# Order of the drain work on four engines of a two-layer transformer kernel, and weight columns that are loaded into another buffer

## What is computed

```
x = x + _L0_attn_ref(_layernorm(x), q_kernel, kv_kernel, out_kernel, q_norm_scale, k_norm_scale)
x = x + _L0_ffn_ref(_layernorm(x), w_gate, w_up, w_down)
x = x + _L1_attn_ref(_layernorm(x), W_K, W_Q, W_V, W_O)
x = x + _L1_ffn_ref(_layernorm(x), W1, W2, W3)
```

## Time and profile before

| | |
|---|---|
| median of 3 runs | 732.27 us (732.14 to 892.83) |
| profiled execution, time | 732.23 us |
| profiled execution, span from first to last instruction | 730.4 us |
| PE busy | 704.2 us, 96% of the span |
| DVE busy | 496.1 us, 68% |
| ACT busy | 403.7 us, 55% |
| POOL busy | 359.0 us, 49% |
| granted TensorE clock | 1.00 |
| DMA | 34 GB/s mean |

### The profile page before, as it was taken

The page is one execution under the profiler, slowest core; times in us unless marked ns, Lnnn a source line. Parts: engine busy times, 40 slices in busy tenths (PEclk is TensorE's granted clock), DMA queues, the critical chain, the costliest instruction groups (busy, mean ns, idle before and its releaser), DMA issues.

```text
span 730.4 us, 14854 instructions
## 1 busy us (share of the span) xinstructions
PE 704.2 (96%) x4296; PEld 628.6 (86%) x4296; DVE 496.1 (68%) x1698; ACT 403.7 (55%) x1205; POOL 359.0 (49%) x508
## 2 busy tenths in 40 slices
PE   4799999999999998999999999999999999999998
PEld 3589999999999987888879999999999999878887
DVE  6998888888888898768757454444445444567443
ACT  4576666666676663523246555555555555554221
POOL 3898888888887884002179342323232325317000
PEclk9999999999999999999999999999999999999999
DMA  6010110101020021100011010101101100000000
GB/s 230 1 44 2 44 45 1 43 0 43 0 101 29 0 87 73 44 1 1 15 59 59 1 59 3 57 14 45 33 25 51 49 0 14 0 15 1 1 30 29
DMA packets 9002, 24.64 MB, mean 34 GB/s; under 512 B 896, under 2 KB 3072, under 8 KB 8832
## 3 DMA queue, kind: packets, MB, share of 16 engines
q1 hardware_dynamic: 8240, 22.55, 8.9%
q10 hardware_dynamic: 720, 1.57, 0.6%
HBM read 23.07 MB, written 1.05 MB: 33 GB/s over the span
## 4 chain that ended last, share of the span: by engine, by line
PE 90%; DVE 6%; issue 1%; POOL 1%; DMA 1%; ACT 1%; DVEq 0%; POOLq 0%; ACTq 0%
PE bank L620 12%; PE bank L309 12%; PE bank L328 11%; PE bank L303 11%; PE bank L360 8%; PE bank L281 7%; PE bank L340 6%; PE bank L349 5%; PE bank L362 4%; PE bank L280 4%; PE bank L371 3%; PE bank L663 2%; PE bank L659 2%; PE bank L687 1%; DVE probs L445 1%
## 5 line engine op out<-in xcount | busy, mean ns | idle before, releaser
L433 ACT ACTIVATE probs<-scores,negmax 128x128 f32<-128x128 f32 (+1 forms) x256 | 115.6, 452 | 43.1 <-DVE negmax L481 42.4
L462 DVE TENSOR_TENSOR enc_lo<-bank,enc_hi 128x256 fp32r<-128x256 f32 x128 | 54.2, 423 | 116.8 <-PE bank L281 110.5
L384 ACT COPY probs_t<-bank 128x384 f32<-128x384 f32 x128 | 61.1, 477 | 120.2 <-PE bank L349 120.2
L525 POOL TENSOR_TENSOR a_hi<-raw_a,zero 128x384 fp32r<-128x384 f32 (+2 forms) x69 | 53.0, 769 | 111.7 <-PE bank L340 108.3
L445 DVE TENSOR_SCALAR probs<-probs,rinv 128x128 f32<-128x128 f32 (+1 forms) x256 | 88.0, 386 | 4.5
L360 PE MATMUL bank<-probs_t,v 128*128 128x256 f32 x256 | 77.1, 383 | 5.1 <-DVE enc_lo L462 4.7
L281 PE MATMUL bank<-qk 128*128 128x256 f32 x256 | 76.5, 381 | 0.0
L538 POOL TENSOR_TENSOR rms_r<-meansq,neg_half 128x3 f32<-128x3 f32 x64 | 58.2, 909 | 34.8 <-DVE meansq L515 34.6
L328 PE MATMUL bank<-b_hi,enc_hi 128*128 128x256 f32 x256 | 74.9, 292 | 0.0
L328 PE MATMUL bank<-b_hi,enc_lo 128*128 128x256 f32 x256 | 72.3, 283 | 0.0
L328 PE MATMUL bank<-b_lo,enc_hi 128*128 128x256 f32 x256 | 72.3, 282 | 0.0
(11 more groups left out here) (124 smaller groups left out, 2032.6 us busy)
## 6 DMA issues: line engine op xcount, KB each, us to landing
raw_a<-in_wa SPq DMA_DIRECT2D x10, 768.0 KB, 4.4
raw_a<-in_wa SPq DMA_DIRECT2D x9, 512.0 KB, 4.0
raw_b<-in_wb SPq DMA_DIRECT2D x16, 256.0 KB, 2.6
x<-in_x SPq DMA_DIRECT2D x4, 256.0 KB, 6.5
w_a<-in_w2t SPq DMA_DIRECT2D x1, 1024.0 KB, 4.9
raw_a<-in_wax SPq DMA_DIRECT2D x2, 512.0 KB, 3.8
raw_b<-in_wdown SPq DMA_DIRECT2D x2, 512.0 KB, 3.8
raw_a<-in_wa ACTq DMA_DIRECT2D x1, 512.0 KB, 5.1
```

Source lines behind the costliest of these rows:

```text
L433: nc.scalar.activation(probs[:, c % 4, c0:c1], scores[:, c % 2, c0:c1], ACT.Exp, bias=negmax[:, c % 2, r:r + 1], scale=-1.0, accum_out=row ...
```

## The change

1. In slots 60 to 70 DVE does `enc_lo` first, ahead of the wait for the scores.
2. The late columns go to `hid_last`, by two DMAs of each layer that SP issues after pair 3 (in layer 1 after a wait for the end of layer 0's feed-forward part), and no longer through `raw_a`; SP's waits for pieces ahead of layer 1's first load fall away or become the wait for "a9".
3. "hi" of the first one or two pieces (two in layer 0, one in layer 1) is made by ACT (`act_early_piece`) at the end of slots 59 and 60, "lo" by POOL in the same slots, before POOL's work of the next slot.
4. Layer 0's pieces 2 and 3 are made by POOL after the last of the norm's powers. Layer 1's pieces 1 and 2 are made between the powers (hi after the powers of tiles 1 and 3, lo after those of 2 and 4), piece 3 after the last.
5. ACT's copies of the Hadamard products stand one slot later.

```diff
@@ dve_slot
             else:
 
+                dve_enc_lo(dve, L, it, c)
                 dve_scores_wait(dve, L, it, c)
                 dve_maxima(dve, L, it, c)
                 dve_normalise(dve, L, it, c)
                 dve_residual(dve, L, it, c)
-                dve_enc_lo(dve, L, it, c)
@@ piece_views
-            if ring == "a":
+            if what in ("x0", "x1"):
+                eng.wait_ge(s_late, 32 * (f + 1))
+                source, dst = hid_last[:, (2 if f == 0 else 1) * slot + src // 512, :], a_w[slot]
+            elif what == "a9":
                 eng.wait_ge(raw_as[f][slot], 16 * (load // 2 + 1))
...
+        def pool_piece_lo(pool, f, n):
+
+            hi, lo, source = piece_views(pool, f, n)
+            pool.wait_ge(ff[f]["whi"], n + 1)
+            nc.gpsimd.tensor_tensor(lo, source, hi.bitcast(F32), ALU.subtract).then_inc(ff[f]["w"], 1)
+
+        def act_early_piece(act, f, n):
+
+            hi, _, source = piece_views(act, f, n)
+            if f == 1:
+                act.wait_ge(ff[0]["up"], 16)
+            nc.scalar.copy(hi, source).then_inc(ff[f]["whi"], 1)
+
         def pool_tail(pool, f):
             def tail(t):
-                n = t + FIRST_TAIL - (LOOP_FROM + LOOP_STEP * LOOPS) - 1
-                if 0 <= n < 4:
-                    pool_piece(pool, f, n)
+                n = t + FIRST_TAIL - (LOOP_FROM + LOOP_STEP * LOOPS)
+                if 0 <= n < (2, 1)[f]:
+                    pool_piece_lo(pool, f, n)
                 if t >= 0:
                     ln_pool(pool, 2 * f + 1, t)
+                if f == 1 and t in (1, 3):
+                    pool_piece_hi(pool, f, (t + 1) // 2)
+                elif f == 1 and t in (2, 4):
+                    pool_piece_lo(pool, f, t // 2)
+                if f == 0 and t == 7:
+                    for n in (2, 3):
+                        pool_piece(pool, f, n)
             return tail
@@ SP
                     if L == 1 and it is None and pair < 2:
-                        need_pieces(sp, 0, f"x{pair}")
+                        if pair == 1:
+                            need_pieces(sp, 0, "a9")
...
+                late = (WA_FFN - WA[L]) // 512
+                if L == 1:
+                    sp.wait_ge(ff[0]["down"], 16)
+                for h in range(2):
+                    sp.dma_start(hid_last[:, late * h:late * (h + 1), :].rearrange("p j t -> p (j t)"),
+                                 wax[L][h]).then_inc(s_late, 16)
...
-                rest = WA_FFN - WA[L]
-                sp.wait_ge(s["a"], 32)
-                sp.dma_start(raw_a[:, 0, 0:rest], wax[L][0]).then_inc(raw_as[L][0], 16)
...
-                need_pieces(sp, L, "a9")
-                sp.dma_start(raw_a[:, 1, 0:rest], wax[L][1]).then_inc(raw_as[L][1], 16)
@@ ACT
                 def tail(t):
+                    n = t + FIRST_TAIL - (LOOP_FROM + LOOP_STEP * LOOPS)
+                    if 0 <= n < (2, 1)[L]:
+                        act_early_piece(act, L, n)
...
-                    if L == 1 and 1 <= t < 5:
-                        act_hadamard(act, t - 1)
+                    if L == 1 and 2 <= t < 6:
+                        act_hadamard(act, t - 2)
```

More of the change, by code:

```diff
@@ L138, in build @@
                     sb("hid_last", [P, 4, 512])]
+        hid_last = hid_late[1]
         work = sb("work", [P, 2560])
@@ L163, in build @@
         ff = [{n: sem(f"F{f}_{n}") for n in fnames} for f in range(2)]
+        s_late = sem("late_columns_loaded")
         s_bf, s_hadmm, s_hadev = (sem(n) for n in ("butterfly", "had_product", "w2_made"))
@@ L981, in piece_views @@
             L = at[f]
-            if ring == "a":
+            if what in ("x0", "x1"):
+                eng.wait_ge(s_late, 32 * (f + 1))
+                source, dst = hid_last[:, (2 if f == 0 else 1) * slot + src // 512, :], a_w[slot]
+            elif what == "a9":
                 eng.wait_ge(raw_as[f][slot], 16 * (load // 2 + 1))
-                if what == "a9":
-                    eng.wait_ge(L["proj"], UNITS)
-                    if f == 1:
-                        eng.wait_ge(L["vproj"], UNITS)
+                eng.wait_ge(L["proj"], UNITS)
+                if f == 1:
+                    eng.wait_ge(L["vproj"], UNITS)
                 source, dst = raw_a[:, slot, src:src + 512], a_w[slot]
@@ L1000, in pool_piece, with pool_piece_hi @@
             split(hi, lo, source, pool, ff[f]["whi"], lambda: pool.wait_ge(ff[f]["whi"], n + 1), ff[f]["w"])
+        def pool_piece_hi(pool, f, n):
+            hi, _, source = piece_views(pool, f, n)
+            nc.gpsimd.tensor_tensor(hi, source, zero[:, 0:1].broadcast_to([P, 512]), ALU.add).then_inc(ff[f]["whi"], 1)
+        def pool_piece_lo(pool, f, n):
[4 more added lines that the diff above has]
+            hi, _, source = piece_views(act, f, n)
+            if f == 1:
+                act.wait_ge(ff[0]["up"], 16)
+            nc.scalar.copy(hi, source).then_inc(ff[f]["whi"], 1)
         def pool_tail(pool, f):
             def tail(t):
-                n = t + FIRST_TAIL - (LOOP_FROM + LOOP_STEP * LOOPS) - 1
-                if 0 <= n < 4:
-                    pool_piece(pool, f, n)
+                n = t + FIRST_TAIL - (LOOP_FROM + LOOP_STEP * LOOPS)
+                if 0 <= n < (2, 1)[f]:
+                    pool_piece_lo(pool, f, n)
                 if t >= 0:
                     ln_pool(pool, 2 * f + 1, t)
+                if f == 1 and t in (1, 3):
[5 more added lines that the diff above has]
+                        pool_piece(pool, f, n)
             return tail
@@ L1122, in _ @@
             slots(pool, 1, pool_slot, pool_head, pool_tail(pool, 1))
-            for n in range(4, len(pieces[1])):
+            for n in range(3, len(pieces[1])):
                 pool_piece(pool, 1, n)
```

## The result

| | before | changed |
|---|---|---|
| median of 22 runs each | 732.33 us | 734.46 us |
| range | 731.47 to 733.72 (one run at 892.83) | 731.89 to 738.09 |
| profiled execution | 732.23 us, span 730.4 | 731.89 us, span 730.1 |
| mean granted clock | 1.000 | 1.000 in the profiled run, 0.998 or less in 14 of 22 |

The changed kernel is 1.0023 times as long (95% interval 1.0013 to 1.0033): 2 us lost where 1 us gained was forecast, and outside the forecast range of 728.6 to 732.9 us. The profiled execution alone would have said otherwise: it is 0.34 us faster. So there are two questions, and the profiled run answers only the first: what each part did, and why the median run is 2.6 us longer than the profiled one.

The account below looks back on a forecast made before the run. PE, busy 704.2 of 730.4 us, was taken as the bound, with at most 7.1 us of idle in the drains to win. 732.23 + 0.5 (layer 0) - 1.45 (layer 1) = 731.3 us, range 728.6 to 732.9.

Parts of the forecast that it names:

- steps 1 to 5: Layer 0's drain: pv wait saved, rotation later, DVE waiting for ACT, stretches returned; 0.5 us lost in all.
- (4): Layer 0's drain, slots 62 to 63: two stretched DVE pairs return 2.48 us; 5.67 us to the pair at 278.2.
- (5): Layer 0, from that pair to the last needed `xT_lo`: 9.16 us before; feed-forward part at 287.8 in place of 287.31.
- steps 6 to 9: Layer 1's drain: earlier pv, later residual add, ACT's hold gone, scalings held up by POOL; 1.45 us gained.
- Step 6: Layer 1's drain: with unit 56's remainder earlier, pv starts at 636.34 in place of 637.74, 1.4 us.
- Step 9: Layer 1's drain: four DVE scalings each wait for POOL's piece operations, 0.8, 1.0, 0.7 and 1.2 us.
- Step 8: Layer 1, slots 64 to 67: later Hadamard copy ends ACT's 2.54 us hold; up to 2.6 us to win.
- Steps 6 and 7: Layer 1: pv 1.4 us earlier, residual add later by some 0.5; slot 64's output product at 644.05, not 644.99.
- What costs nothing: Late columns' DMAs, ACT's second hi and POOL's later pieces, put at no cost; layer 1's pieces ready before PE wants them.
- (B): Slower: DVE's first-placed remainder as head-of-line wait costs layer 0 1.9 us, layer 1 keeps 0.9; 733.2 us, chance 0.15.
- (A): Both drains gain: layer 0 0.6 us in place of its loss, layer 1 2.6; 729.0 us, chance 0.23.
- (C): The change does nothing, the next wait being equally long everywhere; 732.2 us, chance 0.10.

Follow-up runs that it names:

- layer 0 old order: The changed kernel with DVE's encoded remainder last again in layer 0's drain, the new order in layer 1 alone; 731.28 us, ratio 0.9984 to before.

## Why the prediction was wrong

**The view of what bounds it** held but for the clock: all that moved in the stages at full clock, moved in PE's idle time, and every gain and loss is a few tenths to 2.8 us.

**Layer 0, steps 1 to 5.** The mechanism was right row by row. Adding the 0.98 by which this run's head is earlier: the scores of unit 62 at 269.6 (forecast 269.5), DVE's remainder in slot 62 at 272.7 (272.55), the pair of unit 63 at 278.5 (278.2), the feed-forward part at 288.3 (287.8). The loss was 0.98 in place of 0.5. No single term has it: 0.1 us was there by the start of slot 62, (4) took 5.83 us in place of 5.67, and (5) 9.80 in place of 9.6. The two stretches that (4) counted on did go (0.55 us each). POOL's second early piece at 268.23 stretched another pair, that at 268.46, to 1.39 us, but DVE stood idle for 1.50 us behind it, so this cost nothing:

```profile
268.46 1.39 DVE L447 TENSOR_SCALAR probs<-probs,rinv 128x128 f32<-128x128 f32 x2
269.77 0.41 DVE L455 TENSOR_TENSOR x<-bank,x 128x256 f32<-128x256 f32 x1
271.68 0.42 DVE L464 TENSOR_TENSOR enc_lo<-bank,enc_hi 128x256 fp32r<-128x256 f32 x1 [1.50 <-ACT enc_hi L394]
```

The step that I took as half neutral, the remainder first, was the larger loss: undone alone it brings 2.34 us.

**Layer 1, steps 6 to 9.** Gain 2.25 in place of 1.45. Step 6 was right (pv at 636.35, forecast 636.34). Step 9 was too large: DVE's scalings took

```profile
648.77 0.74 DVE L236 TENSOR_SCALAR xn<-x,ln_mv,ln_r 128x256 f32<-128x256 f32 x1
...
651.28 0.73 DVE L236 TENSOR_SCALAR xn<-x,ln_mv,ln_r 128x256 f32<-128x256 f32 x1
...
653.72 0.54 DVE L236 TENSOR_SCALAR xn<-x,ln_mv,ln_r 128x256 f32<-128x256 f32 x1
...
655.42 1.33 DVE L236 TENSOR_SCALAR xn<-x,ln_mv,ln_r 128x256 f32<-128x256 f32 x1
```

against 0.40 alone, 1.74 us over in place of 3.7; one of the four reached 1 us, where my sign of being right asked for three or four. DVE's slots 65 to 67 still began at 647.65, 650.14 and 652.58, near the forecast 647.4, 650.0 and 652.8, so most of what (9) had too much stood there as other work or waits that I had left out. Step 8 was the real gain: I had put it at up to 2.6 us by PE's pace over slots 64 to 67, which holds all three of ACT's waits, and by itself it is worth 2.80. Steps 6 and 7, the order, gave nothing on top of it.

**What costs nothing: the step that failed.** I put the later pieces of layer 1 at no cost, since they are ready when PE wants them, and they were. I did not ask which DVE instructions run beside them. The row of L956 in the kernel before would have told:

```profile
L956 DVE TENSOR_TENSOR enc_lo<-qk,enc_hi x16: 677/685/1775, 672.3 to 723.2; 128x512 fp32r<-128x512 f32 x16
```

Two of its sixteen took 1.57 and 1.78 us, the others 0.68 to 0.69. The two were those that met POOL's last operation. The prediction had named "any new PE idle in the feed-forward parts" as a sign of being wrong, and this is it. I had named the rule on two SBUF inputs, and applied it to layer 0's remainders alone, where it turned out harmless, as said (L896 there took 1.77 us for two against 1.29, and PE waited for nothing new). Layer 1's four remainders have 4.5 us between the hidden tiles and PE; pieces that end 3 us later behind the feed-forward part's start make them 6.4. Cost: 1.90 us, twice the 0.95 us that the sum had as its gain.

**The clock: a second term that was put at nothing.** The forecast was a sum against one profiled execution, and took the clock to stay as it was. The new order of waits in layer 0's drain, 1.11 and 0.66 us with three transposes between, goes with 3.4 us at 1.2 GHz in both profiles that fell, and 29 of the 44 runs with these waits are low. 1.6 us of the 2.4 between the changed kernel's runs at 1.000 (730.1 to 730.8) and most of the low ones (732.4 to 733.3) are that; the other 0.8 may lie in the head: it is 259.9 in the changed kernel's profiled run that kept the clock and 260.5 in the one that did not. Whether the head and the fall belong together is open ("layer 0 old order" kept 2.4 GHz there at a head of 261.4).

**The rivals.** (B) came nearest: slower, and layer 0's head of line waits are its mechanism, but its price was 1.0 and not 1.9, and with layer 1's 2.25 it would give 731.0, not a slower kernel. (A) was half right: a version with the two drains 1.65 and 2.72 us shorter exists, and it is the one without the new order. (C) fell.

## What to carry to other kernels

An operation that waits for another engine should not stand at the head of a slot on the engine that sets the pace, even if a PE wait goes with it: here a wait of 0.84 us went, DVE waited 3.6 us for ACT in its place, and the drain was 2.3 us longer than with the old order. When work is moved off a critical stretch, follow it to where it lands, and list what runs beside it there, by form; an engine that is 50% idle is no proof. Read the granted clock over many runs and not in one profile, and undo each part alone: one edit of five carried 3.4 us by itself, and the others, as they stood together, gave it back.

## What the runs showed of the hardware

TensorE's granted clock fell from 2.4 to 1.2 GHz for 3.4 us behind waits of 0.3 to 1.1 us each that stand close together, in four profiles, and behind one of 1.76 us in a fifth. By the mean clock, 29 of 44 runs of the kernels with waits of 1.11 and 0.66 us are low, and none of 109 with 0.84 and 0.66 us. It fell in some runs of the same kernel and not in others, which moved the median by 2 us and left a single profile unmoved.

DVE's 128x512 subtraction with both inputs in SBUF took 0.69 us alone and 1.59 on average beside POOL's operations of the same shape, which went from 1.04 and 1.29 to 1.49 and 1.62.
